# A four-stage attention pipeline on one core: the first layer's order of work rolled over the pass boundary, and a re-tiled scan

## The reference

```python
# L0: decoder block, 16 heads of 64
x = LN(x + MHA(x, x, x, key mask, causal)); x = LN(x + MHA(x, ctx, ctx, key mask))
x = LN(x + relu(x @ w1 + b1) @ w2 + b2)
# L1: attention of x over ctx, 16 heads of 8, relu on q, k and v, row mask
x = softmax(q k / sqrt(8)) v + x
# L2: linear attention, 8 heads of 16: encoder over 2*ctx, decoder block over x and that encoding, FFNs
# L3: attention of LN(x) over LN(ctx), 8 heads of 16, residual; then a recurrence over the 128 tokens:
s = silu(s @ A.T) + u_t          # s is 32 x 64, u = (LN(x) @ W_in.T + b_in) @ Bmat
out = x + states @ Cmat + mean(program_probs) @ W_prog.T + b_prog
```

## Time and profile before

| | |
|---|---|
| median of 3 runs | 2089.89 us (2089.58 to 2092.27) |
| profiled execution, its own time | 2096.73 us |
| its span, first to last instruction | 2095.0 us |
| busy in the span | PE 1851.6 us (88%), DVE 1332.6 (64%), ACT 1111.3 (53%), POOL 235.2 (11%) |
| chain that ended last | PE 60%, DVE 20%, ACT 14%, issue 4%, POOL 2% |
| mean granted TensorE clock | 0.977 of full speed |

### The profile page before, as it was taken

One profiled execution on the slowest core, in us unless ns is written; L12 is line 12 of the kernel. 1 busy time (PEld: TensorE's weight loads), 2 busy tenths in 40 slices (PEclk: granted clock), 3 DMA queues, 4 the chain that ended last, 5 costly groups with the idle time before them and its releaser, 6 DMA issues.

```text
span 2095.0 us, 36282 instructions
## 1 busy us (share of the span) xinstructions
PE 1851.6 (88%) x13690; PEld 1191.5 (57%) x13690; DVE 1332.6 (64%) x3613; ACT 1111.3 (53%) x3858; POOL 235.2 (11%) x263
## 2 busy tenths in 40 slices
PE   7887999899988999899988999899988998877788
PEld 4555566556655566656655566556655566545344
DVE  5544768567775768567775768567775768564420
ACT  5452845557373845558363845558372845533123
POOL 0001011010212011010212011010212011010100
PEclk9989999999999999999999999999999999998999
DMA  6000000000000000000000000000000000000001
GB/s 194 6 1 6 13 1 1 1 17 2 1 1 7 12 1 1 1 17 1 1 1 6 13 2 1 1 17 1 1 1 6 1 1 1 1 1 1 0 11 31
DMA packets 25714, 20.15 MB, mean 10 GB/s; under 512 B 2307, under 2 KB 23110, under 8 KB 25542
## 3 DMA queue, kind: packets, MB, share of 16 engines
q1 hardware_dynamic: 25320, 17.75, 2.9%
q10 hardware_dynamic: 222, 0.09, 0.0%
HBM read 15.73 MB, written 2.10 MB: 9 GB/s over the span
## 4 chain that ended last, share of the span: by engine, by line
PE 60%; DVE 20%; ACT 14%; issue 4%; POOL 2%; DMA 0%; ACTq 0%; POOLq 0%; DVEq 0%
PE ps L863 16%; PE ps L871 11%; PE ps L913 6%; ACT probs L1539 5%; PE ps L1028 4%; ACT s_probs L1539 4%; PE ps L923 3%; DVE neg_max L1805 3%; PE ps L937 3%; PE ps L859 3%; DVE tok L1825 2%; PE ps L1052 2%; DVE stats L1812 2%; PE ps L909 2%; PE ps L1005 2%
## 5 line engine op out<-in xcount | busy, mean ns | idle before, releaser
L1539 ACT ACTIVATE probs<-ps,neg_max 128x128 f32<-128x128 f32 x1024 | 362.0, 393 | 173.2 <-DVE neg_max L1805 172.9
L1539 ACT ACTIVATION_READ_ACCUMULATOR probs<-ps,neg_max 128x1 f32 x1024 | 238.1, 233 | 0.0
L1805 DVE TENSOR_REDUCE neg_max<-ps 128x4 f32<-128x512 f32 x256 | 164.9, 686 | 113.5 <-PE ps L913 113.5
L1539 ACT ACTIVATE s_probs<-ps,s_max 128x128 f32<-128x128 f32 x672 | 184.0, 400 | 68.1 <-DVE s_max L1805 67.6
L674 POOL TENSOR_TENSOR rstd<-var_eps,minus_half 128x4 f32<-128x4 f32 x88 | 90.2, 1025 | 1059.8 <-DVE var_eps L1818 1059.0
L1812 DVE BATCH_NORM_STATS2 stats<-ps 128x6 f32<-128x128 f32 x352 | 78.2, 285 | 182.2 <-PE ps L871 180.4
L1847 DVE TENSOR_TENSOR probs<-probs,inv 128x512 f32<-128x512 f32 x256 | 183.6, 717 | 8.8
L1533 ACT ACTIVATE probsT<-ps 128x512 f32<-128x512 f32 (+1 forms) x270 | 162.2, 634 | 40.8 <-PE ps L923 28.2
L923 PE MATMUL ps<-ident,probs 128*128 128x128 f32 x1024 | 155.6, 279 | 18.3 <-ACT queries L1533 10.7
L913 PEld LDWEIGHTS ps<-keys,queries 64*128 64x128 f32 x2048 | 127.1, 191 | 55.2 <-issue 55.2
L1533 ACT ACTIVATE kx<-ps 128x512 f32<-128x512 f32 x61 | 36.4, 596 | 218.7 <-PE ps L859 109.8
(11 more groups left out here) (301 smaller groups left out, 3528.3 us busy)
## 6 DMA issues: line engine op xcount, KB each, us to landing
x_in<-in_x SPq DMA_DIRECT2D x8, 256.0 KB, 2.9
c_in<-in_ctx SPq DMA_DIRECT2D x8, 256.0 KB, 3.3
skip_in<-in_mask_BxS_ik SPq DMA_DIRECT2D x8, 256.0 KB, 3.2
out<-headsT SPq DMA_DIRECT2D x28, 64.0 KB, 1.8
w_qkv_sa<-in_L_xattn_sa_wv SPq DMA_DIRECT2D x2, 256.0 KB, 5.5
bv_all_sa<-in_L_xattn_sa_bv SPq DMA_DIRECT2D x2, 256.0 KB, 6.4
w_qkv_ca<-in_L_xattn_ca_wq SPq DMA_DIRECT2D x1, 512.0 KB, 3.4
w_qkv_ca<-in_L_xattn_ca_wk SPq DMA_DIRECT2D x1, 512.0 KB, 4.3
```

The costliest lines, as they stand in the source:

```text
L1539: last = A(dst[:, u % dst.shape[1], h * 128:h * 128 + 128], bank(st, (tag, "s", u))[:, h * 128:h * 128 + 128], ACT.Exp, bias=src_max[:, u ...
L1805: V.tensor_reduce(dst[:, u % 2, :], bank(st, (tag, "s", u)).rearrange("p (h k) -> p h k", h=4), AX.X, ALU.max, negate=True).then_inc(max_r ...
```

## The change

`MAIN_ORDER` ends with `... co7 mk+ y2 r2 n2 f0 f1 f2 f3 y3 r3 i0+ aq0+ ak0+ n3` and starts with `as0 i1 ax0 aq1 ...`: a name with `+` is done for the next group (`placed`), and a pass -1 of `main` alone does these for group 0. The rest of `MAIN_ORDER`, `SIDE_AT` and `LAST_AT` have new values. Bank and count of each fill of `main` now come from a walk over all passes (`main_counts`). Both inputs' copies are ACT's (`i1` was DVE's). The context's copy for `side` moves from `hand_over` to `y3` (`keep_context`), and `i1`'s copy waits for it. The fillers around `n3` go, and the wait after it stays in the eighth group alone. `masks_taken` is signalled after the second mask instead of after all six operations. In `last`, `o` gets bank 4. The recurrence goes by strips of 32 columns.

```diff
-MAIN_ORDER = ("i0 ak0 mk aq0 as0 av00 ak1 i1 ax0 av10 aq1 ax1 at0 as1 av01 av02 at1 ax2 ak2 aq2 av03 at2 as2 "
...
-              "ct10 ct11 cx13 cs7 co5 ct12 cx14 ct13 ct14 cx15 co6 ct15 co7 y2 r2 n2 f0 f1 f2 f3 y3 r3 n3").split()
+MAIN_ORDER = ("as0 i1 ax0 aq1 ak1 av10 ax1 ak2 at0 as1 av00 av11 aq2 at1 ax2 av01 at2 av02 av03 as2 ak3 ax3 "
...
+              "cx13 ct11 cs7 ct12 co5 ct13 cx14 co6 ct14 cx15 ct15 co7 mk+ y2 r2 n2 f0 f1 f2 f3 y3 r3 i0+ aq0+ "
+              "ak0+ n3").split()
-BUSY = {"ln2": 16, "ln3": 16, "end": 12}
+BUSY = {"ln2": 16}
-            by = "AD"[item[-1] % 2]
+            by = "A" if tag == "in" else "AD"[item[-1] % 2]
+def placed(i, step):
+    for item in step:
+        j = Pass(i.g + 1) if item in NEXT_GROUP else i
+        if 0 <= j.g < GROUPS:
+            yield j, item
-                order.append(((tag, "o", (j - 1) // per - 1), 7, "D"))
+                order.append(((tag, "o", (j - 1) // per - 1), 4, "D"))
-LAST_AT = (0, 1, 2, 3, 4, 5, 5, 6, 7, 8, 8, 9, 10, 11, 12, 12, 13, 14, 15)
+LAST_AT = (0, 0, 1, 5, 8, 10, 15, 16, 19, 21, 23, 24, 25, 26, 27, 32, 35, 36, 39)
+            alone(main(Pass(-1)))
             interleave(main(Pass(0)), setup, SETUP_AT)
...
-                            if tag == "ln3":
-                                keep_busy(BUSY["end"], 3)
+                            if tag == "ln3" and i.g == GROUPS - 1:
                                 wait_emptied(pe, i, MAIN, item)
...
+                if st is LAST:
+                    hold(i, LAST, (tag, "o", b))
...
+            def keep_strip(strip):
+                mm(ps[32 * strip:32 * strip + 32, 5, :], ident_h[:, 0:32], ident_h[:, :].unsqueeze(1).broadcast_to([128, 4, 128]),
+                   start=True, stop=True)
             def scan_step(k):
                 if k > 1:
                     pe.wait_ge(scan_silu, k - 1)
-                mm(ps[0:NS, k % 2, 0:B], aT, scan_in[:, k - 1, :], start=True, stop=True).then_inc(scan_mm, 1)
+                for n in range(0, NS, 32):
+                    last = mm(ps[n:n + 32, k % 2, 0:B], aT[:, n:n + 32], scan_in[:, k - 1, :], start=True, stop=True)
+                last.then_inc(scan_mm, 1)
+            def final_step(t):
+                n, dst = final_bank(t)
...
+                mm(dst, scan_in[:, t, :], w_c[:, :], start=True, stop=False)
+                last = mm(dst, x2_all[:, t, :], ident[:, :], start=False, stop=True)
...
             for k in range(1, T):
                 scan_step(k)
-                if k >= 2 and k % 2 == 0:
-                    final_states(k // 2 - 1)
-                elif k >= 2:
-                    final_residual(k // 2 - 1)
-                    keep_half(2, 5)
-                else:
-                    keep_half(3, 5)
+                final_step(k - 1)
+                keep_strip(2 if k % FINAL_STEPS == 0 else 3)
...
+                            if kind == 1 and i.g:
+                                act.wait_ge(context_kept, i.g)
...
+            def keep_context(i):
+                if i.g:
+                    wait_filled(dve, Pass(i.g - 1), SIDE, ("b3", "y"))
+                V.tensor_scalar(c_side[:, :], cT[:, :], 1.0, None, ALU.mult).then_inc(context_kept, 1)
...
+                            if tag == "ln3":
+                                keep_context(i)
...
                 V.tensor_scalar(x_side[:, :], xT["b"][:, :], 1.0, None, ALU.mult)
-                V.tensor_scalar(c_side[:, :], cT[:, :], 1.0, None, ALU.mult)
```

More of the change, by code:

```diff
@@ L527, in wait_all_emptied @@
                 by = st.by[name]
[L528 to L530 removed]
+                last[by] = max(last.get(by, 0), emptied_count(i, st, name))
+            for by, count in last.items():
+                eng.wait_ge(emptied[st, by], count)
         def column_rows(c):
```

149 lines of the change are left out of this document (79 added, 70 removed), and 16 rows, old and new, of tables (MAIN_ORDER, SIDE_AT).

## The result

The kernel after takes 2028.33 us (median of 4 runs, 2023.16 to 2029.39) against 2091.06 (4 runs, 2089.58 to 2092.27) of the kernel before beside it: ratio 0.9695, 95% interval 0.9677 to 0.9714, 62.7 us less. The profiled execution has a span of 2027.1 us at a mean clock of 0.988.

A forecast was written before the change was run, and what follows sets the result against it. PE's own list was taken to bound passes 1 to 7, dependent steps the eighth group, ACT and PE answering each other the recurrence. -12.6 - 4.0 - 0 - 1.5 - 3.5 - 13 + 0 = -34.6: 2055.3 us, range 2030 to 2084.

The forecast's parts named there:

- Boundary with side work: Six boundaries, passes 1/2 to 6/7: PE's idle or filler falls from 5.7 to 3.6 us, 2.1 each, 12.6 in all.
- 0.5 us a pass: Rest of the new order within the passes, trading short PE waits: 3.5 us less in all, bounds -18 to +14.
- Boundary 0/1: Boundary of passes 0 and 1, without side steps: 4.0 us less, bounds 2 to 4.4.
- Boundary 7/8: Boundary into the eighth group: nothing pulled ahead, filler goes, wait stays, steps 84 to 86 later; 0, bounds -1 to +1.5.
- Start: Kernel start: `as0` no longer waits for the last mask operation; 1.5 us less, bounds 0 to 2.
- Eighth group: Eighth group's side layers: attention 24 us less, eleven steps moved into the norm chain 11 more; net 13 less.
- Recurrence: 127 steps of 0.58 us: product in two strips changes a step by -0.04 to +0.06 us; taken as 0.
- side estimate of +3 us: Recurrence, from the skill's 25 ns matmul issue gap: two more pairs add 0.05 us on the tail, save 0.02 at the head.
- Masks, queues, residual at 0: Masks before `y2`, SP's later loads of x and ctx, and POOL's residual after `ln3`'s root: each worth 0.
- ACT's line becomes the bound: Rival: at a pass's start l1's key spreading stands behind exponentials and copies; 6.2 us a pass, 43 us, 2099; chance 0.09.
- The clock: Rival: without filler, the 12 us of PE work at a boundary run at the lower clock; price 84 us, 2139; chance 0.02.
- Saves more: Rival: the new order saves a further 3 us a pass from short waits; 2034; chance 0.07.

The follow-up runs named there:

- without the roll: Kernel after with mk, i0, aq0, ak0 at their own pass's head: 2132.89 us; plus before's fillers 2111.98; plus side steps 85, 86 ahead of n3 2114.91.
- the version without the end wait: Kernel after without PE's wait, at the end of a side pass, for l3's u to be read: 2015.43 us, and 2018.99 us in another session.

## Why the prediction was wrong

- **Boundary with side work, 2.1 us each.** The sequence was right, the wait for L2051's successor stood where it was put (1.44 us, forecast some 1.75), and `as1` came 0.8 us earlier. As a cause it was half right: with the shorter boundary alone a pass is 0 to 1 us shorter, and the gain stays only with the new order. A pass then takes 231.6 us, where the forecast had 233.5. What I priced at "0.5 us a pass" for the order holds the other share. Roll, order, boundaries and start together were 21.6 us by the forecast; what is left of 62.7 without the eighth group (35) and the recurrence (5) is 23, and in the traces the seven passes are 25 to 31 us shorter. That the sum comes near is in part luck, since the split was not right.
- **Boundary 0/1, 4.0.** From `n3` of pass 0 to `n3` of pass 1 it is 228.5 us for 234.3, 5.8 less, in which the new order has its share.
- **Boundary 7/8, "I count 0", bounds -1 to +1.5.** From `n3` to the hand-over it went from 2.7 to 5.0 us, +2.3, beyond the bound: z and u stand behind `n3` there with nothing beside them, at the lower clock.
- **Start, 1.5.** The first scores came 1.7 earlier (13.51 in the earlier trace rows, 11.80 after), and ACT's keys are now waited for; pass 0 kept 0.7.
- **Eighth group, -13: the step that failed.** The attention fell as said (to 50, measured 47.7). The failed term is "the other eleven go into the norm chain ... 1 us each, +11": they cost 1.3, since their work went into the waits of PE and DVE there; the chain, forecast near 63 us, took 52.3. And "the `o` in bank 4 included" priced the bank at nothing of its own, and the second attention at no change; the bank is worth 7.2 us alone and 9.5 to 10.6 with the new places, the clock's share included, as the division no longer holds the next group's head products, and the second attention lost 3.6. The row for it was there, the 5.03 of the earlier trace rows, and I had put all of it down to `ahead` work. Alone these edits are worth 35 us, beyond my bound of 26. How much of that is the clock is an estimate only.
- **Recurrence, "I take 0".** Measured -0.037 a step, 4.7 in all, inside the bounds (-0.04 to +0.06). The argument put up to 80 ns for two more pairs on the tail. The rows show the contrary: the four narrow pairs take 0.26 us from first start to last end (at 1979.86 of the kernel after, and in the row at 1989.86 above) and the two wide ones 0.30, and Silu's idle fell from 0.39 to 0.35; the head stayed at 0.05. The side estimate of +3 us did not come either. What else decides, and was not in the argument, is what streams in the product's strips, or in another width, when Silu ends.
- **Masks, queues, residual at 0:** PE's waits in the seven passes have none for a mask, a load or the residual.
- **Rivals.** "ACT's line becomes the bound" did not come: no wait for `kx` at the start of a pass (PE waits up to 1.5 us for ACT's `keys` once a pass, in the cross-attention), though `cT`, now ACT's, was waited for 2.8 us without the roll. Its price was not the sum of its terms either: 2.8 + 0.6 + 0.7 is 4.1 a pass, not 6.2. "The clock" did not come with the roll and did without it (1.00 against 0.96 from 430 to 1815 us). "Saves more" was the nearest, 2034, but for the wrong stage.

Open stays why identical code takes 1648 or 1654 us for the seven passes of before in different executions, beyond that the clock is lower in the longer one (0.99 against 1.00 from 430 to 1815 us); what the medians of the version without the end wait gained above 6 us; and whether the new order planned for no roll would win anything.

## What to carry to other kernels

Where work is moved from one chain into another, price it by the waits that the other chain has left, not by a flat rate per step: here 5.6 us of PE's work cost 1.3, with all filler kept. Look for a shared bank as its own term: who reads it last, and who wants it next. A step moved across a boundary and the list around it are one edit; test them together before either is credited. After such a move, look for a wait whose cover has gone: here it was one line, worth 6 us in the passes. And before a whole time is credited to an edit, look whether a stage that it cannot touch has moved as well; pass 0 moved by 5 us.

## What the runs showed of the hardware

- Products of 32 columns in different strips run beside each other, and a loop that puts one of 64 columns behind them takes 0.786 us a step against 0.545. Four narrow pairs of load and product took 0.26 us where two wide ones took 0.30.
- A product that PE is given later can start earlier: in the kernel after, the filler (L1524) follows the residual product (L1547) in PE's list and starts 0.21 us ahead of it, in another strip. It does so in the first step too (1953.78 against 1954.00), where no earlier filler can be meant:

```profile
1979.95 0.39 PE L1524 MATMUL ps<-ident_h 128*32 128x512 bf16 x1
1980.16 0.38 PE L1547 MATMUL ps<-ident,x_all 128*32 128x128 f32 x2
```

- Behind an idle of 2.07 us ahead of the eighth group one pair of products ran at full clock and the next at half (1.92 for 1.02); filler in that idle brought 1.00 for the whole group in one profile and 0.96 in the other, against 0.91 and 0.94 without.
